# An attention block on one core: a group's first tail tile moved into the QKV stage, and a second place for the q and k halves

## The reference

```python
h = _layernorm(x) * (1 + ca) + sa
x = x + ga * attention(h, W_qkv, b_qkv, W_proj, b_proj)     # 16 heads, causal, rope
h = _layernorm(x) * (1 + cb) + sb
x = x + gb * _L0_ffn_ref(h, ...)
```

## Time and profile before

| what | us |
|---|---|
| median of 3 runs | 3267.95 |
| lowest and highest run | 3266.17, 3269.23 |
| profiled execution, its own time | 3263.36 |
| its span, first to last instruction | 3261.6 |
| mean granted clock of PE in it | 0.969 |

### The profile page before, as it was taken

How to read it: one execution, slowest core, us unless ns; L and a number is a source line. 1 busy time by engine, 2 the same in 40 slices (tenths; PEclk the granted TensorE clock), 3 DMA queues, 4 the chain that set the end, 5 groups by cost and what they waited for, 6 DMA issues and landing times.

```text
span 3261.6 us, 59116 instructions
## 1 busy us (share of the span) xinstructions
PE 3008.8 (92%) x21664; PEld 1157.1 (35%) x21664; DVE 2491.3 (76%) x4214; ACT 1842.8 (57%) x3651; POOL 1586.5 (49%) x1586
## 2 busy tenths in 40 slices
PE   3699999999999999999999999999999999999896
PEld 1324343434343332434333243433424333342222
DVE  4597777777768788777877878777887878878477
ACT  2406565786655555786555555587555555455541
POOL 2303435382516556272654726366472645627355
PEclk8759999999999999999999999999999999999997
DMA  5403030413031120413114031321314122031121
GB/s 209 110 1 73 14 77 14 99 43 73 17 99 38 47 78 27 103 45 84 44 43 104 30 96 34 68 65 32 97 33 118 40 49 67 28 78 46 56 79 61
DMA packets 180875, 205.27 MB, mean 63 GB/s; under 512 B 21460, under 2 KB 137428, under 8 KB 179428
## 3 DMA queue, kind: packets, MB, share of 16 engines
q1 hardware_dynamic: 180584, 201.50, 23.1%
HBM read 114.09 MB, written 36.50 MB: 46 GB/s over the span
## 4 chain that ended last, share of the span: by engine, by line
PE 41%; issue 20%; DVE 13%; POOL 11%; POOLq 7%; ACT 3%; DVEq 2%; DMA 2%; SPq 1%; ACTq 1%
PE ring L1171 8%; PE ps_out L1221 8%; DVE mpart L911 8%; PE ps_scores L1207 7%; POOL psum L538 5%; PE ps_scores L1145 5%; PE ps_den L1238 4%; PE ps_den L1244 3%; POOL psum L537 3%; PE ring L1193 2%; PE ps_scores L1157 2%; POOLq L573 2%; POOLq L511 2%; POOLq L565 1%; ACT prob L739 1%
## 5 line engine op out<-in xcount | busy, mean ns | idle before, releaser
L739 ACT ACTIVATE prob<-ps_scores 128x512 f32<-128x512 f32 (+3 forms) x2560 | 1251.8, 537 | 950.1 <-PE ps_scores L1210 457.6
L911 DVE TENSOR_REDUCE mpart<-ring 128x1 f32<-128x512 f32 (+3 forms) x2560 | 1406.3, 599 | 356.6 <-PE ring L1171 191.0
L1171 PE MATMUL ring<-qk 96*128 96x512 f16 (+3 forms) x2560 | 875.0, 364 | 64.6 <-DVE mpart L911 46.7
L1207 PE MATMUL ps_scores<-qk 98*128 98x512 f16 (+3 forms) x2560 | 861.9, 350 | 44.4 <-ACT prob L739 36.2
L537 POOL TENSOR_TENSOR psum<-prob 128x512 f32<-128x512 f32 x360 | 480.6, 1335 | 387.2 <-ACT prob L739 305.7
L1221 PE MATMUL ps_out<-prob,v 128*32 128x512 f32 (+3 forms) x5120 | 602.0, 542 | 0.0
L1171 PEld LDWEIGHTS ring<-qk 96*128 96x128 f16 x2560 | 235.5, 98 | 857.6 <-DVE mpart L911 590.2
L538 POOL TENSOR_TENSOR psum<-prob 128x512 f32<-128x512 f32 x360 | 480.4, 1334 | 0.0
L1207 PEld LDWEIGHTS ps_scores<-qk 98*128 98x128 f16 x2560 | 245.8, 98 | 362.7 <-ACT prob L739 227.1
L1145 PE MATMUL ps_scores<-hT,wg 128*128 128x512 f16 x1536 | 346.1, 382 | 4.6 <-POOL hT L528 3.5
L556 POOL TENSOR_TENSOR xs<-xs,bc 128x512 f32<-128x512 f32 x60 | 81.0, 1350 | 432.0 <-DMA xs<-in_L_attn_x_dram 430.7
(11 more groups left out here) (128 smaller groups left out, 2581.9 us busy)
## 6 DMA issues: line engine op xcount, KB each, us to landing
qk<-half SPq DMA_DIRECT2D x384, 128.0 KB, 3.5
turn<-in_rope_dram SPq DMA_DIRECT2D x64, 512.0 KB, 4.6
xs<-in_L_attn_x_dram SPq DMA_DIRECT2D x124, 256.0 KB, 2.8
attn_out_T<-ot SPq DMA_DIRECT2D x63, 256.0 KB, 2.2
otin<-attn_out_T SPq DMA_DIRECT2D x30, 512.0 KB, 4.5
out_dram<-x SPq DMA_DIRECT2D x60, 256.0 KB, 2.1
wg<-w_qkv_halves SPq DMA_DIRECT2D x16, 768.0 KB, 5.1
qk<-in_L_wmod_dram SPq DMA_DIRECT2D x1, 6144.0 KB, 26.8
```

What stands on the lines that cost most here:

```text
L739: act.activation(prob[:, s % 3, p, h % 2, 0:w], ps_scores[(HG * s + h) % NBK][:, 0:w], ACT.Exp, scale=SCALE).then_inc(exp_done, 1)
L911: dve.tensor_reduce(mpart[:, h, qt, kc:kc + 1], ring[use % NBK][:, 0:w], AX.X, ALU.max).then_inc(ring_free, 1)
L1171: mm = pe.matmul(ring[use % NBK][:, 0:w], qk[0:R, G % 2, 0, h, qt * P:(qt + 1) * P], qk[0:R, G % 2, 1, h, kc * QC:kc * QC + w], start=True ...
L1207: mm = pe.matmul(ps_scores[k % NBK][:, 0:w], qk[0:RM, par, 1, h, kt * P:(kt + 1) * P], qk[0:RM, par, 0, h, cq * QC + q0:(cq + 1) * QC], st ...
```

## The change

It has four parts.

- **Two places for the halves.** Even chunks (0 and 2) put their halves into `spare_half`, a part of `prob[:, 2]`; odd ones into `half`. There is a semaphore for each kind and each place, so `high` of a chunk waits for the transfers of the chunk before last. Two more waits guard the spare place: at chunk 0 ACT waits until the group before is through with `prob`, and at step 2 ACT waits for the transfers of the even chunks.
- **The first tail tile of a group** has the position -6. PE's `proj` stands in the QKV stage between chunk 1's q, k and its v; DVE's product at the end of chunk 1, the statistics at the end of chunk 2, the first norm in chunk 3 ahead of the last v copy. POOL's stages 0 and 1 stand ahead of the step loop. What is left, second statistics and last passes, falls on steps 0 and 2.
- **SP's loads for it** move from chunk 2 to chunk 0, behind `rows_load` and ahead of the stack transfers.
- **The other positions:** in groups 0 and 1 they were 2, 8, 16, 24, 30 and are -6, 4, 12, 20, 28; in groups with six tiles 2, 8, 14, 20, 26, 30 become -6, 2, 9, 16, 23, 29. The planner spreads the score units by the new positions.

```diff
-    FIRST_TAIL = 2
+    FIRST_TAIL = -6
...
-            return {s: g * T0 + k for k, s in enumerate((2, 8, 16, 24, 30))}
+            return {s: g * T0 + k for k, s in enumerate((FIRST_TAIL, 4, 12, 20, 28))}
...
-            return {s: 2 * T0 + k for k, s in enumerate((2, 8, 14, 20, 26, 30))}
+            return {s: 2 * T0 + k for k, s in enumerate((FIRST_TAIL, 2, 9, 16, 23, 29))}
...
+        spare_half = prob[:, 2].rearrange("p b h q -> p (b h q)").bitcast(F16)[:, 0:4 * QC].rearrange(
+            "p (k a q) -> p k a q", k=2, a=2)
+        def halves(c):
+            return spare_half if c % 2 == 0 else half
...
-        stack_dma = [sem(f"stack_dma{i}") for i in range(2)]
+        stack_dma = [[sem(f"stack_dma{i}_{j}") for j in range(2)] for i in range(2)]
...
@@ SP, qkv
                     if c == 0:
                         row_load()
+                        tail_load()
                     stack_halves(G, c, 0)
-                    if c == 2:
-                        tail_load()
...
@@ POOL, body, ahead of the steps
+                    if FIRST_TAIL in tail:
+                        t = tail[FIRST_TAIL]
+                        uses[t] = n
+                        n += 1
+                        for stage in range(2):
+                            tail_stage(b - 1, t, stage, uses[t], jobs + t // 2 + (NT // 2 if t >= 2 * T0 and not last else 0))
...
@@ ACT, high
-                act.wait_ge(stack_dma[kind], 48 * (NC_ * G + c))
-                act.copy(half[:, kind, 0, :], xr[:, j % 2, :]).then_inc(hi_done, 1)
+                act.wait_ge(stack_dma[kind][c % 2], 48 * (NC_ // 2 * G + c // 2))
+                if c == 0:
+                    act.wait_ge(prob_used, wait_value(NS * (G - 1)))
+                    act.wait_ge(pair_sum, wait_value(2 * NP * (G - 1)))
+                act.copy(halves(c)[:, kind, 0, :], xr[:, j % 2, :]).then_inc(hi_done, 1)
...
@@ ACT, steps
+                            if s == 2 and h == 0 and nxt:
+                                for kind in range(2):
+                                    act.wait_ge(stack_dma[kind][0], 48 * NC_ // 2 * (G + 2))
...
@@ DVE, qkv
                     turned_sum(G, c, 0)
+                    if c == NC_ - 1:
+                        tail_part(c)
                     if c == NC_ - 1:
                         leave_v(G, c)
...
                         for kind in range(2):
                             low(G, c, kind)
+                        tail_part(c)
...
+                    def tail_part(c):
+                        if FIRST_TAIL in tail and c == 1:
+                            tail_product(b - 1, tail[FIRST_TAIL], n)
+                        elif FIRST_TAIL in tail and c >= 2:
+                            tail_stage(b - 1, tail[FIRST_TAIL], c - 1)
+                            if c == NC_ - 1:
+                                tail_second_row(b - 1, tail[FIRST_TAIL], c - 1)
...
@@ PE, qkv
                     for kind in range(2):
                         qk_job(G, c, kind)
+                    if c == 1:
+                        tail_tile()
                     if c == 0 and before is not None:
                         turn_maxima(before)
                     v_job(G, c)
...
+                    def tail_tile():
+                        if FIRST_TAIL in tail:
+                            pe.wait_ge(max_rows, G + 1)
+                            proj(b - 1, tail[FIRST_TAIL], n)
```

More of the change, by code:

```diff
@@ L269, in adaln_block_kernel @@
                 plan = unit_plan(tail, head)
+                freed_by += ["dve"] * (FIRST_TAIL in tail)
                 for s in range(NS):
@@ L358, in stack_halves @@
                     sp.dma_start(qk[r * HS:(r + 1) * HS, G % 2, kind, :, c * QC:(c + 1) * QC],
-                                 half[:, kind, a, :]).then_inc(stack_dma[kind], 16)
+                                 halves(c)[:, kind, a, :]).then_inc(stack_dma[kind][c % 2], 16)
             def qkv(G, before, row_load, tail_load):
@@ L721, in body @@
                     turns = {}
+                    n += FIRST_TAIL in tail
                     for s, (cq, kt) in enumerate(STEPS):
@@ L884, in low @@
                 dve.wait_ge(hi_done, j + 1)
-                dve.tensor_tensor(half[:, kind, 1, :], xr[:, j % 2, :], half[:, kind, 0, :], ALU.subtract).then_inc(lo_done, 1)
+                dve.tensor_tensor(halves(c)[:, kind, 1, :], xr[:, j % 2, :], halves(c)[:, kind, 0, :], ALU.subtract).then_inc(lo_done, 1)
             def leave_v(G, c):
@@ L892, in leave_v, with qkv @@
                                          ALU.mult, ALU.add).then_inc(v_evac, 1)
-            def qkv(G):
+            def qkv(G, tail_part):
                 for c in range(NC_):
@@ L1017, in _ @@
                 head_normed(0, t)
-            qkv(0)
+            qkv(0, lambda c: None)
             for kind in range(2):
@@ L1030, in body @@
                     nxt = not (last and g == NG - 1)
-                    if nxt:
-                        qkv(G + 1)
                     tail, head, own = tail_at(g, first, last), head_at(g, last), own_at(g, last)
                     plan = unit_plan(tail, head)
+                    def tail_part(c):
[5 more added lines that the diff above has]
+                                tail_second_row(b - 1, tail[FIRST_TAIL], c - 1)
+                    if nxt:
+                        qkv(G + 1, tail_part)
+                    n += FIRST_TAIL in tail
                     for s in range(NS):
@@ L1128, in turn_maxima, with qkv @@
                              ident16[:]).then_inc(max_turned, 1)
-            def qkv(G, before):
+            def qkv(G, before, tail_tile):
                 pe.wait_ge(wg_ld, 32 * (G + 1))
@@ L1168, in unit_scores @@
                     for kind in range(2):
[L1169 removed]
+                        pe.wait_ge(stack_dma[kind][qt // TPC % 2], 48 * (NC_ // 2 * G + qt // TPC // 2 + 1))
                 bank_free(use)
@@ L1256, in _ @@
             pe.wait_ge(head_done, NT)
-            qkv(0, None)
+            qkv(0, None, lambda: None)
             for u in range(NS):
@@ L1266, in body @@
                     nxt = not (last and g == NG - 1)
+                    tail = tail_at(g, first, last)
+                    def tail_tile():
+                        if FIRST_TAIL in tail:
+                            pe.wait_ge(max_rows, G + 1)
+                            proj(b - 1, tail[FIRST_TAIL], n)
                     if nxt:
@@ L1269, in body @@
                             pe.wait_ge(head_done, NT * (b + 2))
-                        qkv(G + 1, G)
+                        qkv(G + 1, G, tail_tile)
                     else:
                         turn_maxima(G)
+                    n += FIRST_TAIL in tail
                     pe.wait_ge(max_rows, G + 1)
```

## The result

The changed kernel takes **3280.1 us** (median of 7 runs, 3274.5 to 3282.9), the kernel before 3268.4 beside it: ratio 1.0038, 95% interval 1.0026 to 1.0049. It is slower by 0.4%, on the other side of the forecast of 3249. The profiled execution has a span of 3278.3 us against 3261.6, 16.7 more.

A forecast was written before the change was run, and what follows sets the result against it. PE, busy 92% of the span, was taken to bound the kernel. The terms summed to -19.2 us: 3263.4 - 19.2 + 4.6 = 3249 us, the forecast's own range 3237 to 3262, the overall range 3222 to 3281.

The forecast's parts named there:

- otin behind bc: Group 0's QKV stage: the attention tile lands behind the modulation rows, PE idles 5.9 us; 17.7 plus 7.5 us of clock.
- That leaves 8.0: Steps of groups 0 and 1: PE's waits per group fall from 11.0 to 8.0 us through the wider spacing.
- of the 7.5 us I keep 4.5: Steps of groups 0 and 1: PE's waits for POOL's pair sums fall from 7.5 to 4.5 us.
- one of three ring waits goes: Steps of groups 0 and 1: the product's 1.6 us wait for a ring bank loses a third, 0.5 us.
- the wait for ACT: Steps of groups 0 and 1: PE's wait for ACT at step 3 goes, at most 0.9 us.
- the +1.4 for DVE in the first steps: Groups 0 and 1: the early tile's later stages fall on steps 0 and 2, when DVE is behind, adding 1.4 us.
- What could be late is the last chunk's v copy ... ACT hides that: End of the QKV stage: the v copy now stands behind the norm, but ACT covers the delay; no cost counted.
- Six-tile steps: Steps of three groups with six tail tiles: -6.5 us each, -19.5 in all, including 2.8 us for late x.
- The second place: Group 0: high copies no longer wait for the last chunk's transfers; 14.9 us go in the steps, -15.5 with QKV idle.
- The product: Nine QKV stages where PE never idles: 12 more matmuls each, 2.59 us a stage, +23.3 us.
- Only the product moves, the waits stay: Rival for the steps: the spacing does nothing and waits only move, +30 us, 3279 us; chance 0.15.
- The other slower one: Rival: late loads in the first steps make PE idle and lose clock, 4.0 us idle in group 1; 3282 us, chance 0.12.

The follow-up runs named there:

- old_spacing: Changed kernel with the tiles inside the steps put back to their old positions, early tile left in the QKV stage: 3275.3 us, ratio 1.0025 to the kernel before.
- both_narrow: Changed kernel with two of POOL's three tail additions and DVE's four norm passes on 8 columns instead of 512, for time alone: 3203.8 us, ratio 0.9811.
- v_first: Changed kernel with DVE making chunk 3's v copy ahead of the first norm's two passes: 3282.4 us, ratio 1.0048 to the kernel before.
- loads_early: Changed kernel with loads of the first tile inside the steps issued at chunk 2 of the QKV stage, ahead of the next group's weights: 3263.9 us, ratio 0.9996.
- rows_early: both_loads with the modulation rows loaded at the last step of the batch before instead of in group 0's QKV stage: 3239.8 us, ratio 0.9921.
- both_loads: Changed kernel with first tail tile's loads ahead of the modulation rows and first in-step tile's loads at chunk 2 of the QKV stage: 3248.4 us, ratio 0.9953.
- POOL's cut: Changed kernel with two of POOL's three additions per tail tile on 8 columns instead of 512, for time alone: 3245.4 us, ratio 0.9934.
- dve_narrow: Changed kernel with DVE's four full-width norm passes per tail tile on 8 columns instead of 512, for time alone: 3223.5 us, ratio 0.9867.
- after: The changed kernel itself, with all four parts and no follow-up edit: 3280.1 us, ratio 1.0038 to the kernel before.

## Why the prediction was wrong

By its terms, from the stretches of the two profiled executions:

| term | forecast | measured |
|---|---|---|
| product in nine QKV stages | +23.3 | +23.4 (9 x 2.60) |
| otin behind bc, with the clock, group 0 | +25.2 | +25.3 (42.4 + 43.4 + 42.4 - 3 x 34.3) |
| otin, six-tile groups | +0.9 | +2.8 (35.3 + 35.3 + 35.1 - 3 x 34.3) |
| steps of groups 0 and 1, with the second place | -48.5 (33.6 + 14.9) | -24.3 (969.2 to 944.9) |
| group 0's QKV idle | -0.6 | -1.5 |
| steps of the six-tile groups | -19.5 | -8.4 (-2.4, +0.8, and -6.8 with the last group) |
| all other stretches | 0 | -0.4 |
| sum | -19.2 | +16.9 (16.7 by the spans; the rest is rounding) |

- *The failed step* is "That leaves 8.0. Bounds: none (PE alone) and 11.0 (spacing does nothing). I take 8.0, nearer to the measured end." Measured: 157.5 - 135.2 - 10.4 = 11.9, above the upper bound. Of its parts, "of the 7.5 us I keep 4.5" became 6.6 (6.0 in batch 1), "one of three ring waits goes" did not come (1.6), the wait for ACT went as forecast, the +1.4 for DVE in the first steps came as the 1.8 for the v copy, and the late otin (0.7 to 1.9 us in group 1) was not in this term. old_spacing shows why the spacing did not pay: it takes 2.4 us from the pair sums, and PE waits for DVE's maxima instead (1.3 becomes 2.9), which the sum had left as they were. both_narrow shows in group 0 what most of the waits are made of, the tail's vector work, which spacing doesn't remove. By the table this row misses by 24.2 of 36.1 us, 2.3 of them by the second place.
- *"What could be late is the last chunk's v copy ... ACT hides that"* was wrong too: PE itself needs the bank that the copy reads, for the scores of step 0. But v_first shows that its 1.8 us are not to be had by order alone.
- *Six-tile steps* (11 us): the mechanism, x late behind the weights, was right in two of the three groups, and loads_early shows it; 2.8 us was too small a price there (5.6 and 7.8 against the third group, 2.3 and 7.0 by loads_early). The third, in the last batch, has no weights to wait behind, which the prediction did not see. The other waits, taken as those of a five-tile group, were too small by 1.3 to 2.1 us (160.5 and 161.3 against 159.2).
- *otin behind bc* was right in order, size and clock. The loss is not all net, though: undone, it brought 16 us and not 25, since the rows then delayed the half stacks: rows_early, which takes the rows out of the stage, is 5.5 us shorter in group 0 than both_loads. The Trainium skill ("DMA: Bandwidth & Descriptors", "Queues, rings and completion order") has descriptors on each engine consumed in ring order, a later one possibly finishing its write first; the 9.1 us of otin agree with the first half, and nothing here shows the second.
- *The second place* was right, 12.6 us in the steps of group 0 instead of 14.9. *The product* was right to 0.1.
- Of the rivals, "Only the product moves, the waits stay" came, at 3279 with a chance of 0.15. That it fits to 1 us is partly luck: it has 17.8 us of waits in all three groups with six tiles, which had 17.9, 20.1 and 12.3 (166.1, 168.3 and 160.5, each less 135.2 and 13.0). The other slower one, PE idle for late loads in group 1, had its mechanism but not its size: 0.7 to 1.9 us for otin instead of 4.0.

What stays open: how the 3.2 us of POOL's cut and the 6.5 of DVE's in group 0 divide into work and mutual delay (together they took 7.9), what the rest of group 1's waits is, and why short half-clock stretches fall into one group's steps and not another's of the same waits.

## What to carry to other kernels

Price a re-spacing by what is left of the work, not by the waits that it is meant to spread: if the same additions and passes run on the same two engines, a wait that one of them loses can turn up at the other, so take today's waits as the value and a full spread as the bound. That fits the groups with five tiles here; in those with six the new positions were worth 0.7 to 5.8 us. When work moves into another stage, its loads move in their queue too, and the two cheap edits here (a load ahead of a large one, a load ahead of the next weights) were worth 28 to 34 us, more than the change itself lost. Run the parts alone: the second place was a gain that the rest of the change hid.

## What the runs showed of the hardware

DVE and POOL hold each other up. In dve_narrow, two passes of the same line on 8 columns, one alone and one beside a POOL addition:

```profile
1906.57 0.22 DVE L978 SCALAR_TENSOR_TENSOR wk<-x,mv,bc 128x8 f32<-128x8 f32 x1
...
1936.61 1.27 DVE L978 SCALAR_TENSOR_TENSOR wk<-x,mv,bc 128x8 f32<-128x8 f32 x1
```

```profile
1936.59 1.26 POOL L545 TENSOR_TENSOR psum<-prob 128x512 f32<-128x512 f32 x1
```

The second started 0.02 us after the addition and ended 0.03 us after its end: 1.27 us instead of 0.22. The other way round, in after, a pair sum that met two norm passes took 1.73 us, its neighbour 1.27:

```profile
1965.06 1.27 POOL L545 TENSOR_TENSOR psum<-prob 128x512 f32<-128x512 f32 x1
1966.29 1.73 POOL L544 TENSOR_TENSOR psum<-prob 128x512 f32<-128x512 f32 x1
```

The Trainium skill ("SBUF — State Buffer", "Who interferes with whom") says that a DVE instruction with two SBUF inputs contends with a GpSimd instruction that reads SBUF; the traces agree, with these numbers. So the cut to 8 columns saved 8.7 us of DVE's busy time in a group (133.75 to 125.08), not the 16 to 20 that I had put down. I had priced a pass at its mean in the steps (1.21 us) without asking what it takes alone: 0.75, as in the two norm passes shown above, beside which POOL had nothing to do.
